# Graph attention on one core: the work of a graph ordered in halves, VectorE masking heads in twos

## What is computed

```python
q, k, v = (proj(Wq, bq), proj(Wk, bk), proj(Wv, bv))      # x @ W.T + b, split in 8 heads of 32
scores = jnp.einsum('bhqd,bhkd->bhqk', q, k) * SCALE       # SCALE = 32 ** -0.5
scores = scores * (adj_matrix + bond_matrix)[:, None, :, :]   # both are adj here
attn = jax.nn.softmax(scores, axis=-1)
ctx = jnp.einsum('bhqk,bhkd->bhqd', attn, v)
out = jnp.einsum('bse,fe->bsf', ctx, Wo) + bo
x = _layernorm(x + out, axis=-1)
```

## Time and profile before

| | |
|---|---|
| time, median of 3 runs | 583.24 us (579.94 to 585.08) |
| the profiled execution's own time | 583.36 us |
| its span, first to last instruction | 581.6 us |
| busy PE / DVE / ACT / POOL | 76% / 72% / 64% / 42% of the span |
| DMA moved | 94.14 MB, mean 162 GB/s |

### The profile page before, as it was taken

How to read it: one execution, slowest core, us unless ns; L and a number is a source line. 1 busy time by engine, 2 the same in 40 slices (tenths; PEclk the granted TensorE clock), 3 DMA queues, 4 the chain that set the end, 5 groups by cost and what they waited for, 6 DMA issues and landing times.

```text
span 581.6 us, 12230 instructions
## 1 busy us (share of the span) xinstructions
PE 439.7 (76%) x3604; PEld 318.9 (55%) x3604; DVE 417.6 (72%) x1717; ACT 371.0 (64%) x1222; POOL 247.1 (42%) x379
## 2 busy tenths in 40 slices
PE   8777779777778777778767679767778877776665
PEld 7545556555556555556555456555556655554444
DVE  5756687677686686786777677786787777677874
ACT  4775666675676666766666666675676676676650
POOL 3215234354361642635445352643544364232354
PEclk9988898888899788998799888897998888899877
DMA  6664565665755757566565746766575574754661
GB/s 236 181 159 149 118 176 164 163 183 133 233 122 147 189 141 212 129 176 167 140 192 139 225 120 167 200 158 188 132 191 155 131 199 106 212 130 107 173 165 65
DMA packets 60004, 94.14 MB, mean 162 GB/s; under 512 B 7969, under 2 KB 49186, under 8 KB 59938
## 3 DMA queue, kind: packets, MB, share of 16 engines
q1 hardware_dynamic: 46610, 68.19, 47.4%
q10 hardware_dynamic: 13328, 25.17, 12.7%
HBM read 26.22 MB, written 8.39 MB: 60 GB/s over the span
## 4 chain that ended last, share of the span: by engine, by line
PE 37%; DVE 33%; issue 13%; ACT 13%; ACTq 1%; DMA 1%; POOL 1%; SPq 0%; DVEq 0%; POOLq 0%
DVE probs L453 19%; PE row_bank L243 16%; PE ctx_bank L351 10%; ACT probs L636 7%; PE proj_bank L290 6%; DVE boxes L471 6%; DVE context L486 3%; PE turn_bank L260 3%; ACT kq L657 3%; DVE low_top L462 3%; ACT inverse L650 3%; DVE mean_var L504 1%; DMA w_whole<-in_wv 1%; ACTq L629 1%; DVE top L453 1%
## 5 line engine op out<-in xcount | busy, mean ns | idle before, releaser
L636 ACT ACTIVATE probs<-probs,low_top 128x256 f32<-128x256 f32 x512 | 255.4, 501 | 186.8 <-DVE low_top L462 186.8
L453 DVE CUSTOM_DVE_ANT_0 probs<-row_bank,adj_rows 128x256 f32<-128x256 f32 x512 | 192.8, 413 | 137.8 <-PE row_bank L243 137.4
L290 PE MATMUL proj_bank<-xt_parts,w_parts 128*128 128x512 f32 x360 | 128.8, 486 | 85.3 <-ACT kq L657 85.3
L290 PEld LDWEIGHTS proj_bank<-xt_parts,w_parts 128*128 128x128 f32 x360 | 71.4, 221 | 128.4 <-ACT kq L657 91.3
L471 DVE STREAM_TRANSPOSE boxes<-probs 128x512 f32<-128x512 f32 x192 | 135.2, 705 | 0.0
L243 PE MATMUL row_bank<-kq 32*128 32x256 f32 x1024 | 94.0, 492 | 12.5 <-DVE top L453 12.3
L769 POOL CAST ctx_parts<-context 128x512 fp32r<-128x512 f32 x31 | 18.9, 609 | 186.5 <-DVE context L486 186.5
L636 ACT ACTIVATION_READ_ACCUMULATOR probs<-probs,low_top 128x1 f32 x512 | 96.7, 189 | 0.0
L243 PEld LDWEIGHTS row_bank<-kq 32*128 32x128 f32 x1024 | 56.6, 224 | 43.4 <-issue 39.2
L260 PE MATMUL turn_bank<-ident,probs 128*128 128x128 f32 x256 | 40.3, 281 | 33.6 <-ACT inverse L650 33.6
L351 PE MATMUL ctx_bank<-carried,v_boxed 128*32 128x256 f32 x760 | 63.6, 398 | 0.0
(11 more groups left out here) (74 smaller groups left out, 485.0 us busy)
## 6 DMA issues: line engine op xcount, KB each, us to landing
carried<-boxes SPq DMA_DIRECT2D x256, 192.0 KB, 3.8
adj_rows<-in_adj ACTq DMA_DIRECT2D x16, 512.0 KB, 3.5
v_boxed<-v SPq DMA_DIRECT2D x128, 64.0 KB, 2.2
xr<-in_x ACTq DMA_DIRECT2D x16, 512.0 KB, 6.1
out<-result ACTq DMA_DIRECT2D x31, 256.0 KB, 2.2
xt<-in_x_t SPq DMA_DIRECT2D x15, 512.0 KB, 3.7
xt<-in_x_t SPq DMA_DIRECT2D x2, 256.0 KB, 3.3
w_whole<-in_wk ACTq DMA_DIRECT2D x2, 128.0 KB, 3.5
```

The costliest lines, as they stand in the source:

```text
L290: last = nc.tensor.matmul(proj_bank[:], w_parts[:, a, which, t, c * P:(c + 1) * P], xt_parts[:, pair % 2, b, t, :], start=(half_ == 0 and ...
L453: last = nc.vector.tensor_tensor_reduce(probs[:, h % RING, t * S:(t + 1) * S], row_bank[j][:, t * S:(t + 1) * S], adj_rows[:, (g // 2) % 2 ...
L636: last = nc.scalar.activation(tile, tile, ACT.Exp, bias=low_top[:, g % 2, J * c + j, t:t + 1], accum_out=sums[:, g % 2, t, j * T + c:j * T ...
```

## The change

No instruction of the computation is added or taken away, and no tile is new. What changes is the order within `step` on PE, DVE, ACT and POOL:

- PE: weigh_v goes from the end of the step, where it served graph g-1, to the place behind rows(2g) and the first k or q piece, and serves graph g-2. Rows(2g+1) comes ahead of the whole second piece and no longer between its halves.
- DVE: a group's heads are masked in twos, with both `lower_top` behind the two. Box is no longer three heads behind but a group: box(n-1, 0) between the two twos of group n, box(n-1, 1) behind the second, and box(n-1, 2) behind other work. scale_context(g-2) comes after the first group's masks, add_residual(g-2) after the second's, row_stats follows it in the same step, and divide(g) is the last of step g; before, divide(g-1) stood at place 2 of step g.
- ACT: read_kq of a step's first piece is at place 7 of the step before; the second piece is read at place 3, right behind copy_v, with copy_inverse behind it. move_turned goes from places 2 and 7 to 1 and 5.
- POOL: spread_shares(g-1) is first in the step and cut_context(g-2) at place 3.

```diff
@@ PE, step(g)
                 if is_pair(ahead):
                     for half_ in range(2):
                         project_kq(ahead, 2 * (g % 2), half_)
+                if is_graph(g - 2):
+                    weigh_v(g - 2)
                 if is_group(2 * g - 1):
                     turn_probs(2 * g - 1)
                 if is_graph(g + 1):
                     project_v(g + 1)
-                if is_pair(ahead):
-                    project_kq(ahead, 2 * (g % 2) + 1, 0)
                 if is_graph(g):
                     rows(2 * g + 1)
                 if is_pair(ahead):
-                    project_kq(ahead, 2 * (g % 2) + 1, 1)
+                    for half_ in range(2):
+                        project_kq(ahead, 2 * (g % 2) + 1, half_)
                 if is_graph(g - 1):
                     turn_shares(g - 1)
                 if 0 <= g - 2 < LAST:
                     project_out(g - 2)
                 if is_group(2 * g):
                     turn_probs(2 * g)
-                if is_graph(g - 1):
-                    weigh_v(g - 1)
@@ DVE
-            def step(g):
-                for s in range(H):
-                    n, j = 2 * g + s // J, s % J
+            def mask_group(n):
+
+                for j in range(J):
                     if is_group(n):
                         reduce_rows(n, j)
-                        lower_top(n, j)
-                    behind = H * g + s - LAG
-                    if is_group(behind // J) and behind % J < BOXED:
-                        box(behind // J, behind % J)
...
-                    if s == 1 and 0 <= g - 2 < LAST:
-                        scale_context(g - 2)
-                    if s == 2 and is_graph(g - 1):
-                        divide(g - 1)
-                    if s == 3 and 0 <= g - 3 < LAST:
-                        for t in range(T):
-                            row_stats(g - 3, t)
-                    if s == 4 and 0 <= g - 3 < LAST:
-                        aggregate(g - 3)
-                    if s == 7 and 0 <= g - 2 < LAST:
-                        add_residual(g - 2)
+                    if is_group(n) and j % 2 == 1:
+                        for lowered in (j - 1, j):
+                            lower_top(n, lowered)
+                    if is_group(n - 1) and j % 2 == 1:
+                        box(n - 1, j // 2)
+
+            def step(g):
+                mask_group(2 * g)
...
+                if 0 <= g - 2 < LAST:
+                    scale_context(g - 2)
+                if is_group(2 * g - 1):
+                    box(2 * g - 1, 2)
+                if 0 <= g - 3 < LAST:
+                    aggregate(g - 3)
+                mask_group(2 * g + 1)
+                if 0 <= g - 2 < LAST:
+                    add_residual(g - 2)
+                if is_group(2 * g):
+                    box(2 * g, 2)
+                if 0 <= g - 2 < LAST:
+                    for t in range(T):
+                        row_stats(g - 2, t)
+                if is_graph(g):
+                    divide(g)
@@ ACT, step(g)
-                    if s == 1 and g == 0:
+                    if s == 0 and g == 0:
                         copy_v(0)
+                        read_kq(1, 0)
...
-                    if s == 2 and is_pair(ahead):
-                        read_kq(ahead, 2 * (g % 2))
-                    if s == 2 and is_group(2 * g - 1):
+                    if s == 1 and is_group(2 * g - 1):
                         move_turned(2 * g - 1)
...
                     if s == 3 and is_graph(g + 1):
                         copy_v(g + 1)
-                    if s == 5 and is_graph(g - 1):
+                    if s == 3 and is_pair(ahead):
+                        read_kq(ahead, 2 * (g % 2) + 1)
+                    if s == 3 and is_graph(g - 1):
                         copy_inverse(g - 1)
-                    if s == 5 and is_pair(ahead):
-                        read_kq(ahead, 2 * (g % 2) + 1)
-                    if s == 7 and is_group(2 * g):
+                    if s == 5 and is_group(2 * g):
                         move_turned(2 * g)
+                    if s == 7 and is_pair((g + 1) // 2 + 1):
+                        read_kq((g + 1) // 2 + 1, 2 * ((g + 1) % 2))
@@ POOL, step(g)
-                    if s == 0 and g % 2 == 1 and is_pair(g // 2 + 2):
+                    if s == 0 and is_graph(g - 1):
+                        spread_shares(g - 1)
+                    if s == 1 and g % 2 == 1 and is_pair(g // 2 + 2):
                         cut_x(g // 2 + 2, 1)
-                    if s == 1 and 0 <= g - 2 < LAST:
+                    if s == 3 and 0 <= g - 2 < LAST:
                         cut_context(g - 2)
-                    if s == 3 and is_graph(g - 1):
-                        spread_shares(g - 1)
```

More of the change, by code:

```diff
@@ L33 @@
 BOXED = J - 1
-LAG = 3
 LAST = B - 1
@@ L580, in _ @@
                 read_first_q(c)
-            def step(g):
-                for s in range(H):
-                    n, j = 2 * g + s // J, s % J
+            def mask_group(n):
+                for j in range(J):
                     if is_group(n):
                         reduce_rows(n, j)
-                        lower_top(n, j)
-                    behind = H * g + s - LAG
-                    if is_group(behind // J) and behind % J < BOXED:
-                        box(behind // J, behind % J)
-                    if g == 0 and s == 2:
-                        low_weights(3)
-                    if g == 0 and s == 3:
-                        dve.wait_ge(bias_made, 1)
-                        nc.vector.tensor_copy(bias[:], ctx_bank[:, 0:E]).then_inc(bias_ready, 1)
-                    if s == 1 and 0 <= g - 2 < LAST:
-                        scale_context(g - 2)
-                    if s == 2 and is_graph(g - 1):
-                        divide(g - 1)
-                    if s == 3 and 0 <= g - 3 < LAST:
-                        for t in range(T):
-                            row_stats(g - 3, t)
-                    if s == 4 and 0 <= g - 3 < LAST:
-                        aggregate(g - 3)
-                    if s == 7 and 0 <= g - 2 < LAST:
-                        add_residual(g - 2)
@@ new lines, in mask_group @@
+                    if is_group(n) and j % 2 == 1:
[5 more added lines that the diff above has]
+                mask_group(2 * g)
+                if g == 0:
+                    low_weights(3)
+                    dve.wait_ge(bias_made, 1)
+                    nc.vector.tensor_copy(bias[:], ctx_bank[:, 0:E]).then_inc(bias_ready, 1)
+                if 0 <= g - 2 < LAST:
[14 more added lines that the diff above has]
+                    divide(g)
```

## The result

| | before | after |
|---|---|---|
| median of 4 runs | 583.58 us | 463.01 us (457.93 to 470.9) |
| ratio to before, 95% interval | 1 | 0.7879 (0.7804 to 0.7953) |
| profiled execution, its span | 583.36, 581.6 us | 470.9, 469.1 us |

The change takes a fifth off the time. Runs of this kernel differ among themselves by 2.8%, those of before by 0.9%.

The account below looks back on a forecast made before the run. DVE's own work of 12.7 us a graph was to bound the kernel, with ACT's loop about as high; plus 0.3 for carried blocks, 13.0. In us, 26 + 390 + 6.2 + 26.5 + 1.8 = 450, range 430 to 500.

Parts of the forecast that it names:

- Rows no longer wait: PE reaches each group's rows while DVE does other work, so DVE's 3.5 us of idle time a graph is covered.
- The cushion of about 0.9 us: Slack at PE's rows: what DVE's 2.2 us of other work behind the first half's masks leaves beyond the rows.
- One graph costs DVE 12.7 us: DVE's work without waits: 13.2 us a graph from the timeline, less 0.5 us saved by masking heads in twos.
- Divide as a loop through ACT: DVE's divide needs ACT's last exp, and the next masks queue behind it: a loop of 12.4 to 13.0 us a graph.
- The heavy form of this rival: DVE stands 1.5 to 2 us at divide because ACT's k or q read comes late: 14.7 us a graph, 502 us; 13%.
- The context chain: From weigh_v through scale_context and cut_context to project_out on PE: project_out waits 0.4 us, inside PE's 0.5 us to spare.
- Carried blocks: Boxes moved by DMA for weigh_v on PE: median landing passes, longest costs 2.7 us; 0.3 us a graph taken.
- Clock: PE's idle times of 3.02 and 1.89 us go, none over 1 us stays, so full clock is counted.
- the lower-clock rival: Many short pauses of PE keep TensorE at its 1.2 GHz level and PE bounds: 699 us; chance 3%.
- Start and end: Group 2's first mask at 26 us (25 to 28) for 27.00; from group 63 to the end 26.5 us, as before.
- signs of being right: First masks 13.0 us apart, DVE busy above 90%, row wait near nothing, PEclk nines and tens, PE's named waits under 1 us.
- the rule against the DVE term: On DVE the next operation starts only with the pipeline empty: 2.6 us more, 15.6 a graph, 528 us; no chance given.

## Why the prediction was right

The time forecast was 450 us in a range of 430 to 500; 463.0 was measured. Taken step by step:

- *Rows no longer wait.* Right. DVE's wait for rows fell from 137.4 to 13.2 us, and first masks of undisturbed graphs follow without one. The cushion of about 0.9 us held too: half a piece (0.8 us) put back ahead of rows(2g+1) was not felt.
- *One graph costs DVE 12.7 us.* Oversized. With divide out of the way the undisturbed graph is 11.95 us. I had 13.2 less 0.5 for the twos. The runs show 12.93 us with the heads one by one, 0.3 below the 13.2 of the stretches before, and 1.0 us saved by the twos, twice what I had; a two costs 1.56 us where I had 1.66.
- *Divide as a loop through ACT.* Right in kind and size: 12.4 to 13.0 was forecast, 12.3 measured, and moving divide brought the graph to 11.95. This loop, and not DVE's work alone, bounds the undisturbed graph, by 0.4 us. The heavy form of this rival, 14.7 us, did not come: in the undisturbed graph shown ACT found the second piece ready. Over the whole run it waited 26.2 us for PE's pieces, but only 7.7 us in the kernel without the loads, so most of that follows from the late landings.
- *The context chain.* Right: project_out waited 6.6 us in 20 graphs, 0.3 each, inside PE's slack.
- *Carried blocks.* The step that failed. I allowed 0.3 us a graph, took 7.0 us for the longest landing and looked for the wait at weigh_v. The longest landing was 9.5 us, and what stood was the box of two groups later, which needs the same landing for its buffer, and which the prediction passed over: 24.9 us in 7 places, against 6.1 us in 2 places at weigh_v. In the profiled run the graphs are 1.3 us longer in the mean than an undisturbed one (13.6 less 12.3); the experiment without the loads puts what they cost at 0.8 us a graph.
- *Clock.* Half right. In the undisturbed windows, with PE idle for 0.6 us at most at a time, the clock was 1.00, and the lower-clock rival did not come. But I had counted on no idle time over 1 us. Six of the seven waits of box left PE idle for 2.9 to 5.3 us, each time with rows of 2.09 us behind it; in the one shown above the slow matmuls cost 2.8 us more, 9.5 us instead of 6.7 for half a graph.
- *Start and end.* Group 2 came at 27.0 instead of 26, the end took 469.1 - 441.0 = 28.1 us instead of 26.5: 2.6 us together.

Two of the signs of being right did not come either: DVE was busy 85% and not above 90%, and PEclk has sevens and eights. And a sign of being wrong did, in the disturbed graphs: in one of 15.5 us DVE stood 1.75 us ahead of a first mask (at 254.73), since the slow matmuls brought the rows late.

So the mechanism of rows and halves was right, but that the sum came so near is in part luck, because two errors have opposite signs: the undisturbed graph 0.4 us shorter than the 12.7 that I took, the disturbances 1.3 us in the profiled run, and in one of the median's length about 1.0 ((463.0 - 1.8 - 27.0 - 28.1) / 30.5 = 13.3 a graph), instead of 0.3. The graph of 13.0 us hardly exists: nearly all are of 12.3 or of 14 to 17. The spread of the runs fits this, since how many graphs are disturbed depends on when transfers meet: the run of 470.9 us had a mean clock of 0.945, the one of 457.93 us 0.976. Only one of the four was profiled, so it is not shown. The clusters are no matter of that one run: they stand as well in the profile of the half piece alone, taken in a run of 459.48 us, with eight graphs of 14 us and more.

As for the rule against the DVE term, of the Trainium skill's "VectorE: DVE Perf Modes", "The DRAIN you can't avoid": the changed kernel's graph of 12.3 us is far from the 15.6 that waiting for an empty pipeline would give, and the timeline after again has a mask start 0.63 us (263.52 to 264.15) behind a box of 0.71. The section also says that a next operation that is not held starts earlier; I had left that out of the rule, and by it the page and the trace need not differ.

## What to carry to other kernels

Ask of every instruction that feeds the bounding loop which wait stands ahead of it in its own queue. Moving a consumer of far transfers one graph later (weigh_v) was worth 99 us by its own reversal; moving a reader from place 2 of its step to place 7 of the one before (read_kq), together with the half piece, was worth 58 us. When a loop gets shorter, list every place that needs a transfer's landing, the one that frees its buffer as well as the one that reads its data, and set each against the longest landing, not the median; the longest may grow too, here from 7.0 to 9.5 us. A further gain may first have to be bought with a buffer: the same edit lost 10 us with two buffers and full bursts, and won 15 us with four buffers and halved ones. Before a single instruction's saving is priced, look which loop bounds: the twos saved DVE 1.0 us a graph, of which 0.6 showed.

## What was not expected of the hardware

- Landings of SBUF-to-SBUF blocks of 192 KB, 3.9 us in the median, stretched to 9.5, while the DMA share was 0.72 to 0.82 in windows of a graph or two; in the kernel with the later divide and two buffers the longest was 11.0. A share below one over such a window did not tell of bursts of some microseconds.
- The same four transfers of 1.75 MB (transposed x, store, adj, x) went with a wait of box of 2.7 to 5.0 us when they left within 4.5 us, and with none when the first left 2 us sooner.
- In a two no wait stands ahead of the first lower_top. The pair of them started 0.34 us behind the last mask (262.98 to 263.32 in the timeline after) and took 0.20 us of DVE, against the 0.12 of wait and 0.14 of work that I had put there.
